# Cross-attention and feed-forward on one core: scores of two slots in one stretch, softmax steps one slot earlier

## The chip, the cores and the metric

The kernel runs on one core of one Trainium2 chip. The metric is the device time of one execution in microseconds (us). Before the change the median of three runs is 498.65 us (498.59 to 500.09).

## What is computed

For each of 8 batches with 512 rows of 256 features, and a context of 1024 rows of 256 of which a mask leaves a short window:

```python
q = (layernorm(x) @ w_q), k = (ctx @ w_k), v = (ctx @ w_v)     # 16 heads of 64
attn = softmax(where(mask, -inf, q @ k.T / 8))
x = x + (attn @ v) @ w_o
w = quantised_int4(kernel)
x = x + layernorm(x) @ w + bias + (layernorm(x) @ a) @ b
```

All of it is in float32 in the reference. The mask is the same for all query rows and hides all but the last keys, so a window of 160 keys per batch (128 and a rest of 32) is enough; the kernel checks this at run time and has a general path that is not taken here.

## The kernel before, in words

Float32 precision is made from float16 halves: a matrix is split into a high half and a low half, and a product is three matmuls (high by high, high by low, low by high). A high half is ScalarE's copy out of PSUM, a low half VectorE's subtraction behind it.

**Slots.** The work is cut into slots. A batch has 16 slots (u = 0 to 15): 4 tiles of 128 rows by 4 groups of 4 heads. 8 batches make LAST = 128 score slots; 12 more slots drain the tail. Every engine goes through the slots in its own function slot(s), one after the other (fast_sp L506, fast_pool L568, fast_act L635, fast_dve L745, fast_pe L919). The engines' queues are in the order of the code; semaphores join them. So the order in which an engine meets its work is written out by hand.

**What a slot k holds before the change.**
- TensorE (L1078): scores(k+2), 12 matmuls of 64 contraction rows by 160 columns in six concurrent pairs (L997), which wait for exponentials of slot k because there are two PSUM buffers for scores; weighted_values(k-3), 16 matmuls of 65 columns (L929, L1018), which wait for the transposed probabilities and for the normalisation of slot k-4, since there is one output bank; then the slot's projection items and its late items.
- VectorE (L885): normalise(k-4) (L878, L879); the first projection item of slot k-1; maxima(k+1) (L812, L816); the other items of slot k-1 (low halves L794, L805, L785, L788; late items L846, L850, L859 to L867, L871).
- ScalarE (L723): the second layer norm's x2 if there is one (L727), exps(k+1) (L682, four activations), then the high halves of slot k's items (L653, L656, L661, L673, L696, L699). exps(k+1) waits for the split of slot k-1.
- GpSimd (L603): split_probs(k), four instructions (L589, L590, L593, L595); in every fourth slot (group 2) the power, the shift and the sum with the bias of a tile's second layer norm (L611, L613, L614), behind VectorE's statistics of the same slot; once a batch a gather and a power for the first layer norm.
- SP (L525): turn_probs(k), the transpose by DMA of the split probabilities into one of TURN_BUFS = 4 buffers, which waits for the weighted values of slot k-4; loads and stores.

The scores, maxima and exponentials of slots 0 to 3 are made ahead of slot 0, between the first projections.

**Items.** Projections for the next batch and late work of older tiles go through three PSUM banks in turn (p_item, LANES = 3): an item waits until the item three before it was evacuated by VectorE (claim, L932). PROJ (L374) lists projections by u: c and x (transposes of the gathered context and of x), k, q, v; FIRST_PROJ is the list of the first batch; h, r0 and r1 come once in four batches. LATE (L384) gives the late items: in group 0 n (transposes of x2), in group 1 w (24 matmuls with w_o), in group 2 f (the feed-forward, 6 matmuls) and o0, in group 3 o1 (transposes of the attention output). VectorE's part of w, here called the w tail, is the residual sum and the tile's statistics.

## Time and profile before

| | |
|---|---|
| median of 3 runs | 498.65 us (498.59 to 500.09) |
| the profiled execution | 499.79 us |
| its span from first to last instruction | 496.5 us |
| mean granted TensorE clock | 0.977 of full speed |
| TensorE busy, matmuls | 449.6 us (91%) |
| VectorE busy | 403.6 us (81%) |
| GpSimd busy | 398.5 us (80%) |
| ScalarE busy | 328.1 us (66%) |

A busy time counts instructions in flight. Matmuls are pipelined and their ends are modelled, so a gap between two matmuls is better read from their starts. A row of a timeline with "x12" is a run of 12 instructions from the start of the first to the end of the last. A bracket at the end of a row gives the idle time before it and the instruction that ended the wait. Slots are numbered here by their place in the kernel: the score group that TensorE computes in slot k is that of slot k+2, and the start of a slot is the start of that group.

### The profile page before, as it was taken

Reading aid. Unit: us, or ns where it says so; the run is one execution under the profiler, and the core shown is the slowest. Engines: PE = TensorE matmul, PEld = TensorE weight load, DVE = VectorE, ACT = ScalarE, POOL = GpSimd, SP = SyncE. Lnnn points to the kernel's source line nnn. Section 1 sums busy time; section 2 is a strip of 40 time slices with the busy share of each in tenths; the row PEclk is TensorE's granted clock in tenths of the full one; section 3 lists DMA queues with packets and bytes.
Section 4 is the critical chain, followed back from the end, with each engine's and each line's share of the span. In section 5 each row is a group of like instructions: output and inputs, shape, how many; then the busy total and the mean of one; then the engine's idle time right before and its main releaser. Section 6 shows DMA issues by size and latency. Waiting matters only on the chain.

```text
span 496.5 us, 15468 instructions
## 1 busy us (share of the span) xinstructions
PE 449.6 (91%) x5855; PEld 326.8 (66%) x5855; DVE 403.6 (81%) x1110; ACT 328.1 (66%) x845; POOL 398.5 (80%) x659
## 2 busy tenths in 40 slices
PE   3777989999999999999999999999999999888884
PEld 1344756786766866777766866687667876566672
DVE  5886689987988989787988989888988888777762
ACT  5977566866577766776677766776677666655621
POOL 5787478999888978788788988798787977889941
PEclk9899799999999999999999999999999999999897
DMA  8602776697957996689758975899777976769971
GB/s 292 207 23 43 141 171 119 127 204 152 172 118 144 197 142 118 125 185 157 147 120 138 196 155 117 150 172 167 139 132 125 164 153 123 146 113 180 165 122 37
DMA packets 218817, 71.91 MB, mean 145 GB/s; under 512 B 202785, under 2 KB 216882, under 8 KB 218738
## 3 DMA queue, kind: packets, MB, share of 16 engines
q1 hardware_dynamic: 217680, 69.25, 73.0%
q0 software_dynamic: 480, 1.31, 0.9%
q8 instruction: 49, 0.80, 0.6%
q10 hardware_dynamic: 578, 0.30, 0.2%
q14 instruction: 30, 0.25, 0.2%
HBM read 14.71 MB, written 4.19 MB: 38 GB/s over the span
## 4 chain that ended last, share of the span: by engine, by line
PE 43%; DVE 26%; ACT 17%; POOL 8%; issue 4%; DMA 1%; DVEq 0%; POOLq 0%; ACTq 0%
PE ps_b L929 32%; ACT arena L682 8%; DVE ps_a L812 7%; PE ps_a L997 6%; DVE arena L805 4%; DVE arena L794 2%; ACT arena L661 2%; DVE arena L879 2%; POOL arena L589 2%; PE ps_b L1055 2%; POOL arena L593 2%; PE ps_b L1018 2%; ACT arena L633 1%; ACT arena L673 1%; DVE arena L816 1%
## 5 line engine op out<-in xcount | busy, mean ns | idle before, releaser
L929 PE MATMUL ps_b<-arena 128*128 128x65 f16 (+3 forms) x3324 | 320.8, 249 | 7.7 <-DVE arena L879 3.4
L929 PEld LDWEIGHTS ps_b<-arena 128*128 128x128 f16 x3324 | 222.0, 99 | 83.1 <-issue 6.4
L682 ACT ACTIVATE arena<-ps_a,arena 128x160 f32<-128x160 f32 x512 | 160.4, 397 | 92.6 <-DVE arena L816 84.1
L593 POOL TENSOR_TENSOR arena<-arena 128x512 f16<-128x512 f32 x128 | 147.9, 1155 | 0.0
L589 POOL CAST arena<-arena 128x512 f16<-128x512 f32 x128 | 78.0, 610 | 54.7 <-ACT arena L682 52.8
L812 DVE TENSOR_REDUCE ps_a<-ps_a 128x4 f32<-128x640 f32 x128 | 105.3, 823 | 0.0
L997 PE MATMUL ps_a<-arena 64*128 64x160 f16 x1536 | 76.5, 233 | 13.2 <-ACT arena L682 13.1
L997 PEld LDWEIGHTS ps_a<-arena 64*128 64x128 f16 x1536 | 50.9, 95 | 38.2 <-issue 20.9
L1018 PE MATMUL ps_b<-arena 128*128 128x65 f16 x512 | 72.1, 194 | 0.0
L879 DVE TENSOR_TENSOR arena<-ps_b,arena 128x256 f32<-128x256 f32 x128 | 54.3, 424 | 4.4
L805 DVE TENSOR_TENSOR arena<-ps_b,arena 128x512 f16<-128x512 f32 x60 | 41.1, 686 | 19.2 <-ACT arena L673 17.8
L699 ACT ACTIVATE arena<-ps_b 128x512 f16<-128x512 f32 x64 | 38.6, 603 | 26.4 <-PE ps_b L1055 26.4
L595 POOL TENSOR_TENSOR arena<-arena 128x128 f16<-128x128 f32 x128 | 54.5, 426 | 0.0
L590 POOL CAST arena<-arena 128x256 f16<-128x256 f32 x128 | 51.1, 399 | 0.0
L1018 PEld LDWEIGHTS ps_b<-arena 128*128 128x128 f16 x512 | 50.4, 99 | 0.0
L846 DVE TENSOR_TENSOR arena<-ps_b,arena 128x512 f16<-128x512 f32 x64 | 43.9, 686 | 5.7 <-DVE mask_u L871 1.0
L673 ACT ACTIVATE arena<-ps_b 128x512 f16<-128x512 f32 x58 | 35.0, 604 | 16.6 <-PE ps_b L929 15.5
L1055 PE MATMUL ps_b<-ident,arena 128*128 128x128 f32 x256 | 38.6, 274 | 0.6 <-DVE arena L879 0.5
L1055 PEld LDWEIGHTS ps_b<-ident,arena 128*128 128x128 f32 x256 | 30.2, 141 | 5.6 <-issue 0.8
L611 POOL TENSOR_TENSOR arena<-arena,neg_half 128x1 f32<-128x1 f32 x32 | 17.7, 552 | 17.4 <-DVE arena L867 17.1
L878 DVE RECIPROCAL arena<-ps_b 128x4 f32<-128x4 f32 x128 | 22.2, 174 | 3.0 <-PE ps_b L1018 2.7
L816 DVE TENSOR_SCALAR arena<-ps_a 128x4 f32<-128x4 f32 x128 | 20.7, 162 | 4.4
(142 smaller groups left out, 423.0 us busy)
## 6 DMA issues: line engine op xcount, KB each, us to landing
arena<-in_x_dram SPq DMA_DIRECT2D x8, 512.0 KB
mask_u<-in_x_dram SPq DMA_DIRECT2D x32, 128.0 KB, 2.9
out_dram<-mask_u SPq DMA_DIRECT2D x32, 128.0 KB, 2.7
arena<-arena SPq DMA_TRANSPOSE x128, 4.0
arena<-arena SPq DMA_DIRECT2D x24, 65.0 KB, 2.7
arena<-in_L_xattn_w_q_dram SPq DMA_DIRECT2D x1, 1024.0 KB, 8.4
arena<-in_L_xattn_w_k_dram SPq DMA_DIRECT2D x1, 1024.0 KB, 10.4
arena<-in_L_xattn_w_v_dram SPq DMA_DIRECT2D x1, 1024.0 KB, 12.0
```

The lines of the kernel that those rows point to most:

```text
L589: nc.gpsimd.tensor_copy(hi_main, main).then_inc(p_hi_made, 1)
L590: nc.gpsimd.tensor_copy(rests[:, :, 0:2, :], rest.unsqueeze(2).broadcast_to([P, GROUP, 2, REST])) \
L593: nc.gpsimd.tensor_tensor(lo_main, main, hi_main, ALU.subtract)
L595: nc.gpsimd.tensor_tensor(rests[:, :, 2, :], rest, rests[:, :, 0, :], ALU.subtract).then_inc(p_lo_made, 1)
L682: ins = nc.scalar.activation(probs[k % 2][:, h, :], p_scores[k % 2][:, h % 2, h // 2 * WINDOW:(h // 2 + 1) * WINDOW], ACT.Exp, bias=neg_ma ...
L805: ins = nc.vector.tensor_tensor(f_q[par][:, 1, j, :], bank[:, :], f_q[par][:, 0, j, :], ALU.subtract)
L812: link(nc.vector.tensor_reduce(p_max[k % 2].rearrange("p (i e) -> p e i", e=2), p_scores[k % 2][:, :, 0:2 * WINDOW].rearrange("p e (i k) - ...
L879: nc.vector.tensor_tensor(attn[k // NG % 2][:, k % NG * GROUP * DH:(k % NG + 1) * GROUP * DH] .rearrange("p (h d) -> p h d", h=GROUP), out ...
L929: mm = nc.tensor.matmul(dst, a, c, start=(first and at == 0), stop=(last and at == n - 1))
L997: mm = nc.tensor.matmul(p_scores[k % 2][:, e, i * WINDOW:(i + 1) * WINDOW], f_q[par][own, q_half, m, t * P:(t + 1) * P], f_k[par][own, k_h ...
L1018: mm = nc.tensor.matmul(dst, turn[:, 2, e, :], vr[par][:, h, :], start=False, stop=True)
L1055: mm = nc.tensor.transpose(bank[:, m * P:(m + 1) * P], attn[tile % 2][:, c * P:(c + 1) * P], ident[:, :])
```

## The change

Scores: TensorE computes scores(k+2) and scores(k+3) one after the other in every even slot k, none in odd slots. Maxima, exponentials, splits and transposes of a slot are moved ahead by one slot, each on its own engine: in slot k VectorE makes maxima(k+2), ScalarE exps(k+2), GpSimd split_probs(k+1), SP turn_probs(k+1). Weighted values stay where they are. A fifth buffer for transposed probabilities is added. The waits inside scores, maxima, exps, split_probs and turn_probs are unchanged.

```diff
@@ -44,7 +44,7 @@
     R = lora_a.shape[1]
     ST, KT, DT, HT = S // P, K // P, D // P, HD // P
     NG = H // GROUP
-    PV_BEHIND, HALF_BUFS, TURN_BUFS = 3, 3, 4
+    PV_BEHIND, HALF_BUFS, TURN_BUFS = 3, 3, 5
     SCALE = DH ** -0.5
     F_EXP = SCALE / (WS * WS)
 
@@ -523,8 +523,10 @@
                     sp.dma_start(vr[batch % 2][REST * i:REST * (i + 1)], src[rows]).then_inc(vr_loaded[batch % 2], 16)
 
             def slot(s):
-                if s.k < LAST:
-                    turn_probs(s.k)
+                if s.k == 0:
+                    turn_probs(0)
+                if s.k + 1 < LAST:
+                    turn_probs(s.k + 1)
                 if s.k == 0:
                     sp.wait_ge(keep_made, 1)
                     sp.wait_ge(zeros_made, 5)
@@ -601,10 +603,10 @@
             norm(2)
 
             def slot(s):
-                if s.k < LAST - 1:
-                    split_probs(s.k)
-                if s.k == LAST - 2:
-                    split_probs(LAST - 1)
+                if s.k == 0:
+                    split_probs(0)
+                if s.k + 1 < LAST:
+                    split_probs(s.k + 1)
                 tile = s.k // NG - 2
                 if s.g == 2 and 0 <= tile < NT:
                     pool.wait_ge(t_var_made, tile + 1)
@@ -726,8 +728,8 @@
                         act.wait_ge(t_rstd_made, tile + 1)
                         nc.scalar.activation(x2, x1, ACT.Identity, bias=t_shift[:, :], scale=t_rstd[:, :]) \
                             .then_inc(x2_made, 1)
-                if DEEP - 1 <= s.k < LAST - 1:
-                    exps(s.k + 1)
+                if DEEP - 2 <= s.k < LAST - 2:
+                    exps(s.k + 2)
                 if s.k == 4:
                     act.wait_ge(ffn_made, 1)
                     nc.scalar.activation(f_ffn_hi, ffn_w[:, :, :], ACT.Copy).then_inc(split_hi, 1)
@@ -890,8 +892,8 @@
                 if b:
                     for i, name in enumerate(b.proj[:first]):
                         item(b, i, name)
-                if DEEP - 1 <= s.k < LAST - 1:
-                    maxima(s.k + 1)
+                if DEEP - 2 <= s.k < LAST - 2:
+                    maxima(s.k + 2)
                 if s.k == 1:
                     ffn_grid(dve)
                 if s.k == 3:
@@ -1076,8 +1078,9 @@
                 mm.then_inc(item_made, 1)
 
             def slot(s):
-                if DEEP - 2 <= s.k < LAST - 2:
+                if DEEP - 2 <= s.k < LAST - 2 and s.k % 2 == 0:
                     scores(s.k + 2)
+                    scores(s.k + 3)
                 if 0 <= s.k - PV_BEHIND < LAST:
                     weighted_values(s.k - PV_BEHIND)
                 for i, name in enumerate(s.proj):
```

## Rows read from the trace of the kernel before

**Rows 1.** Busy time by stretch: us, TensorE, weight loads, VectorE, ScalarE, GpSimd, clock, DMA.

```profile
50.00:450.00 400.00, 383.47 (x5204) 284.00 (x5203) 340.02 (x935) 271.60 (x736) 333.44 (x563) 0.99 0.80 148
```

**Rows 2.** Timeline, TensorE, slots 45 to 49: start us, us, line, operands, count [idle <-releaser].

```profile
200.64 2.78 PE L929 MATMUL ps_b<-arena 128*128 128x256 f16 x24
...
203.35 0.59 PE L997 MATMUL ps_a<-arena 64*128 64x160 f16 x12
...
203.87 0.26 PE L929 MATMUL ps_b<-arena 128*128 128x65 f16 x3
...
212.52 0.44 PE L1069 MATMUL ps_b<-ident,arena 128*128 128x128 f32 x2 [0.63 <-DVE arena L846]
```

**Rows 3.** Timeline, TensorE, slots 50 and 51 (u = 2, 3) to the start of 52.

```profile
217.03 0.59 PE L997 MATMUL ps_a<-arena 64*128 64x160 f16 x12
...
217.55 0.26 PE L929 MATMUL ps_b<-arena 128*128 128x65 f16 x3
...
218.04 0.63 PE L955 MATMUL ps_b<-ident,arena 128*128 128x128 f32 x4
...
218.51 0.82 PE L929 MATMUL ps_b<-arena 128*128 128x256 f16 x6
...
219.70 0.59 PE L997 MATMUL ps_a<-arena 64*128 64x160 f16 x12
...
220.72 1.82 PE L929 MATMUL ps_b<-arena 128*128 128x160 f16 x24
...
222.91 0.59 PE L997 MATMUL ps_a<-arena 64*128 64x160 f16 x12
```

**Rows 4.** Waits, whole span: engine, line, releaser: us in total, times, longest.

```profile
PEld ps_a L997 <- issue: 20.9, 99, 1.0
```

**Rows 5.** Timeline, TensorE, slot 60 (u = 12).

```profile
251.19 0.25 PE L929 MATMUL ps_b<-arena 128*128 128x65 f16 x3 [0.48 <-DVE arena L879]
```

**Rows 6.** Timeline, TensorE, first score matmuls of slots 6 and 18.

```profile
64.87 0.59 PE L997 MATMUL ps_a<-arena 64*128 64x160 f16 x12 [1.12 <-ACT arena L682]
...
103.74 0.59 PE L997 MATMUL ps_a<-arena 64*128 64x160 f16 x12
```

**Rows 7.** Timeline, GpSimd, near the end of the score work.

```profile
439.26 0.55 POOL L611 TENSOR_TENSOR arena<-arena,neg_half 128x1 f32<-128x1 f32 x1 [2.08 <-DVE arena L867]
...
440.71 0.61 POOL L589 CAST arena<-arena 128x512 f16<-128x512 f32 x1
...
443.11 0.61 POOL L589 CAST arena<-arena 128x512 f16<-128x512 f32 x1
```

**Rows 8.** Timeline, VectorE, slots 50 and 51.

```profile
216.50 0.82 DVE L812 TENSOR_REDUCE ps_a<-ps_a 128x4 f32<-128x640 f32 x1
...
217.47 0.42 DVE L859 SCALAR_TENSOR_TENSOR arena<-ps_b,mask_u 128x256 f32<-128x256 f32 x1
...
218.74 0.17 DVE L878 RECIPROCAL arena<-ps_b 128x4 f32<-128x4 f32 x1
...
219.34 0.69 DVE L785 TENSOR_TENSOR arena<-ps_b,arena 128x512 f16<-128x512 f32 x1
...
219.95 0.82 DVE L812 TENSOR_REDUCE ps_a<-ps_a 128x4 f32<-128x640 f32 x1
...
220.92 0.42 DVE L871 TENSOR_TENSOR mask_u<-ps_b,arena 128x256 f32<-128x256 f32 x1
...
221.49 0.69 DVE L846 TENSOR_TENSOR arena<-ps_b,arena 128x512 f16<-128x512 f32 x1
```

**Rows 9.** Timeline, ScalarE, slot 50.

```profile
217.55 1.25 ACT L682 ACTIVATE arena<-ps_a,arena 128x160 f32<-128x160 f32 x4 [1.16 <-DVE arena L816]
...
218.71 0.60 ACT L653 ACTIVATE arena<-ps_b 128x512 f16<-128x512 f32 x1
```

**Rows 10.** Timeline, VectorE, slot 60.

```profile
250.41 0.17 DVE L878 RECIPROCAL arena<-ps_b 128x4 f32<-128x4 f32 x1
...
250.62 0.42 DVE L879 TENSOR_TENSOR arena<-ps_b,arena 128x256 f32<-128x256 f32 x1
```

## The prediction

> **What bounds the kernel now.** I read the busy times by stretch first, then TensorE's instructions in order of time, then the two engines that feed it, then the end.
>
> By stretch: from 50 to 450 us TensorE has a matmul in flight for 383.5 of 400 us, VectorE is busy 340, GpSimd 333, ScalarE 272 [rows 1]. TensorE sets the pace there, but its busy share hides small gaps, so I went on by the starts of its instructions.
>
> In order of time, a score group (12 matmuls) stands once in every slot, between other matmuls. The group at 203.35 lasts 0.59 us, of which its last matmul takes about 0.23, so its 12 starts lie in 0.36, or 0.066 a pair; a seventh pair could start at 0.40, but the weighted values start at 0.52: leaving the group costs 0.12. The 24 matmuls of 256 columns before it take 2.71 from first start to the group's first start; matmuls of 256 columns start 0.109 apart inside the run (2.78 us less the last one's 0.28, by 23), so 24 need 2.62 or 2.63, and entering costs 0.08 [rows 2, 3]. One round trip is 0.20 us; the list of waits has TensorE's weight loads idle 20.9 us before 99 score groups with no releaser, 0.21 each [rows 4]. Apart from that, TensorE stands still at two places of a batch: at the start of a batch (u = 0), where it waits 0.63 us for VectorE's low half of o1, about 1.6 with the gaps around it [rows 2]; and at u = 12, where the weighted values wait 0.54 us for the normalisation before [rows 5]. Thus about 2.15 us of a batch are waits; two batches take 113.3 us (slot 18 at 103.74 to slot 50 at 217.03, [rows 3, 6]), one of the two with the extra items of a quad.
>
> After 440 us it is GpSimd: four instructions of a split take 2.40 us (440.71 to 443.11), the three of a tile's variance 1.45 (439.26 to 440.71), one after the other to the last split [rows 7]; that stretch begins with a wait of 2.08 us.
>
> **The change, part by part.** Times of a slot count from the first score matmul in TensorE's slot; slot 2 of a batch is the worked example.
>
> *Drains.* 62 even slots hold two groups back to back: 62 x 0.20 = 12.4 us less work for TensorE. The second group costs 0.40 to 0.42. The page "TensorEngine Tiling (Array Packing)" of the Trainium skill, section "Tiling Modes", says that changing the tiling mode drains TensorE; rows 2 and 4 agree, and by that rule alone the time would fall by these 12 us.
>
> *What the shift does to VectorE and ScalarE.* Maxima, exponentials, splits and transposes move by one slot together, so their order among each other stays, and the fifth buffer keeps the transposes waiting for the same weighted values as before: no cost there. GpSimd's gather and the two powers of a batch come one split later; they are covered by its idle time, 67 of 400 us [rows 1], some 0.57 a slot, and would cost up to one split (2.40) a batch if a gather came too late. SP issues one transpose more ahead of the first batch's rest values, which weighted values need only in slot 3; later the order on SP is the same. Not so against the scores. Before, maxima found scores that were a slot old: in the example they start at 216.50, 0.53 us *before* the slot's scores [rows 3, 8]. After it, in even slots they need the scores of the same slot, and cannot start before 0.59 + 0.03 = 0.62. On VectorE the second half of all items of the slot before, the normalisation of the next slot and everything behind it stand in line after that wait; on ScalarE every high half of the slot stands behind the exponentials. VectorE's head start of about 1.1 us is gone in every even slot. And odd slots now begin with weighted values, which need that normalisation 0.52 us sooner.
>
> Slots 2 and 3 [rows 3, 8, 9]. VectorE: maxima 0.62, next instruction 0.97 later (1.59), the w tail 1.27 (2.86), the normalisation 0.63 (250.41 to 251.04, [rows 10]) and 0.15 to TensorE (251.04 to 251.19, [rows 5, 10]) = 3.64. TensorE is there at 2.67 + 0.41 - 0.08 = 3.0, so it waits 0.63. ScalarE: exponentials 1.05 after the maxima (216.50 to 217.55), at 1.67, the x1 half 1.16 behind them, 2.84 to 3.44; VectorE's x1 half 3.47 to 4.16; TensorE wants its bank at 4.14 (weighted values 0.49) and gets it at 4.31: 0.17. Maxima 4.08, f 5.05, bank of f free at 5.60; TensorE has k0 (0.83) done at 5.14 and starts k1 at 5.75: 0.61. With k1 and o1 slot 4 begins at 7.1. Before, the pair took 5.88 (217.03 to 222.91). Cost: +1.2 us.
>
> The other pairs by the same steps, after against before: (4,5) 6.52 for 6.72; (6,7) 6.20 for 6.34; (8,9) 7.45 for 7.65; long TensorE items cover VectorE there, and they keep the drain. (10,11) 6.98 for 6.34: w tail and statistics stand behind the maxima, TensorE waits 0.55, 0.15 and 0.13. (12,13) 7.83 for 8.19, the old wait of 0.54 falling to 0.37. (14,15) 6.37 for 6.36. (0,1) 6.97 for 7.32: the wait for o1 stays, since the chain of high half, low half, maxima, exponentials through v0 and v1 is the same; the wait for exponentials becomes one of 0.4 for the normalisation. Together +0.55 us a batch: waits rise from 2.15 to 4.3, drains fall by 1.6. From slot 18 to 112, 5.9 batches and once more a (2,3) pair: **+3.7 us**.
>
> *First batch.* Its projections are packed differently, and slots 8, 10, 14 have little for TensorE in an even slot, so the normalisation is late in slots 9, 11, 13 and 15 (1.4, 1.2, 0.6, 1.1), the second group of slots 6 and 16 waits for exponentials (1.3, 0.75), and 1.0 goes in small ones: 7.4 us, against 2.9 before and 1.2 of drains saved. The stretch from slot 6 to slot 18, 64.87 to 103.74 [rows 6], becomes 42.2 instead of 38.9 us: **+3.3**. Before slot 6 I find +0.1: the exponentials of slot 2 delay the high halves, but VectorE's own work was the limit.
>
> *End.* Where GpSimd is the limit it enters with one split more done: -2.4. The variance of slot 114 comes 0.4 later, since the w tail stands behind maxima, and one group of 1.45 falls behind split 123 rather than ahead of it, but the last tile's statistics can come only after split 127, and the matmuls after them wait for that. **-2.5 us**; nothing and -3.5 are its ends.
>
> Sum: +3.7 + 3.3 + 0.1 - 2.5 = +4.6. The profiled execution took 499.8 us (span 496.5, 3.3 around it), so 504.4 for it; it lies 1.1 above the median of the runs, so I forecast **503.3 us**. The added waits in this sum are 4.6 + 2.5 + 55 x 0.20 = 18.1 us (seven of the 62 drains lie in the last batch, where GpSimd is the limit, and count for nothing). With none of them the time is 485.2, with twice as many 521.4; those are the outer bounds. I take the worked value, since each wait is a sum of measured durations in an order that the code fixes.
>
> **Rivals.** *One: the drains win, because TensorE reaches VectorE's late work later than I think.* Place: the first weighted values and the second and third bank in slots 3 and 11. If half of those waits and of the first batch's arise, 503.3 - 0.5 x (1.4 + 0.8) x 6 - 0.5 x 7.4 = 493; it is faster than before from the point where 4.6 of the 18.1 us of added waits stay away, a quarter of them. For it: VectorE is busy only 85% [rows 1], and slots 5, 9, 13 leave it time. Against: the slack is in other slots than the waits. The Trainium skill's rule of the drain ("TensorEngine Tiling (Array Packing)", section "Tiling Modes") stands for this rival. Chance 0.27.
>
> *Two: the parts cancel*, 498.65 within 0.3%, about what a measurement of this kernel can tell from no change: the waits of slot 3 shrink to half and the end keeps its gain. Chance 0.13.
>
> *Three: worse*, 508 or more: ScalarE, late in each even slot, passes its delay on through the next maxima, or the end brings nothing. Chance 0.08, and the forecast itself 0.52.
>
> *Four: the change does not do what it says*, the second group waiting in mid-stretch for its exponentials in most slots, so that no drain is hidden: I find that only in slots 6, 16 and the last batch; it is inside three.
>
> **How the numbers follow.** Forecast 500.2 to 508 with 0.52, rival one 487 to 497 with 0.27, two 0.13, three 0.08. Rival one lies below 493 with about 0.1, so 493 to 508 leaves out under 0.2; the forecast's own range is 500.5 to 508. Slower by over 0.3% is 0.60, within 0.13, faster 0.27.
>
> **What would show it.** Right: score groups of 24 matmuls about 0.93 us long; no 0.2 us idle in odd slots; in slots u = 3 and u = 11 weighted values waiting for L879 and the next items for VectorE; maxima in even slots not before L997 of the same slot; batches about 0.55 us longer; GpSimd's last split about 2 us sooner after slot 113. Wrong: batches shorter by 1 us or more, or odd slots that begin without a wait.

## The result, and the profile after

The change made the kernel slower: 513.49 us median of 4 runs (512.86 to 514.86) against 499.37 us (498.59 to 501.02, 4 runs on the same chip), ratio 1.0286, 95% interval 1.0257 to 1.0315. The profiled execution took 514.86 us, with a span of 511.6. All times of parts below are from profiled executions.

Busy time of the kernel after by stretch, in the columns of [rows 1]:

```profile
50.00:450.00 400.00, 369.70 (x5003) 276.55 (x5004) 334.00 (x903) 263.26 (x718) 323.89 (x546) 0.99 0.75 143
```

Every engine is busy less than in [rows 1]: TensorE 369.7 of 400 us for 383.5, VectorE 334.0 for 340.0. Nothing became the bound by work; the time went into waiting. Waits of the kernel after, whole span (engine, line, releaser: us in total, times, longest; "..." marks rows, and in the diffs lines, that are left out):

```profile
ACT arena L684 <- DVE arena L818: 138.8, 121, 3.7
...
DVE ps_a L814 <- PE ps_a L999: 35.6, 37, 2.2
PEld ps_b L931 <- issue: 32.2, 45, 1.7
PE ps_b L931 <- DVE arena L881: 22.4, 36, 1.5
...
PEld ps_a L999 <- issue: 12.1, 61, 0.4
```

The last line answers to [rows 4]: the idle time before score groups fell from 20.9 us before 99 groups to 12.1 before 61, so about 9 us of drains did go. The other lines are what came instead. VectorE's maxima (L814) wait 35.6 us for scores, a wait that the kernel before did not have; ScalarE's exponentials (L684) wait 138.8 us for the maxima, 84.1 before; the weighted values (through the helper, L931) wait 22.4 us for the normalisation (L881), 3.4 before; in the pair shown next, the weight loads' wait without a releaser (32.2 us in all) stands in front of the same weighted values.

One steady pair shows it: slots 66 and 67 (u = 2, 3), the ones that the prediction worked out. TensorE in order of time, the columns of [rows 3], from w of slot 65 to the scores of slot 68:

```profile
282.00 2.79 PE L931 MATMUL ps_b<-arena 128*128 128x256 f16 x24 [0.42 <-DVE arena L781]
...
284.72 1.00 PE L999 MATMUL ps_a<-arena 64*128 64x160 f16 x24
285.66 0.26 PE L931 MATMUL ps_b<-arena 128*128 128x65 f16 x3
...
287.28 0.60 PE L1057 MATMUL ps_b<-ident,arena 128*128 128x128 f32 x4
288.39 0.25 PE L931 MATMUL ps_b<-arena 128*128 128x65 f16 x3 [0.51 <-DVE arena L881]
...
290.30 1.00 PE L931 MATMUL ps_b<-arena 128*128 128x160 f16 x12 [0.36 <-DVEq L875]
...
291.67 1.00 PE L999 MATMUL ps_a<-arena 64*128 64x160 f16 x24
```

VectorE in the same two slots, as in [rows 8], and then ScalarE, as in [rows 9]:

```profile
285.36 0.83 DVE L814 TENSOR_REDUCE ps_a<-ps_a 128x4 f32<-128x640 f32 x1 [1.01 <-PE ps_a L999]
...
286.34 0.42 DVE L861 SCALAR_TENSOR_TENSOR arena<-ps_b,mask_u 128x256 f32<-128x256 f32 x1
...
287.61 0.17 DVE L880 RECIPROCAL arena<-ps_b 128x4 f32<-128x4 f32 x1
...
288.19 0.69 DVE L787 TENSOR_TENSOR arena<-ps_b,arena 128x512 f16<-128x512 f32 x1
```

```profile
286.42 1.25 ACT L684 ACTIVATE arena<-ps_a,arena 128x160 f32<-128x160 f32 x4 [2.26 <-DVE arena L818]
287.54 0.61 ACT L655 ACTIVATE arena<-ps_b 128x512 f16<-128x512 f32 x1
```

The 24 score matmuls stand in one run, 0.94 us to the next instruction where two groups took 2 x 0.52. But the maxima start 0.64 after the run began (285.36 - 284.72), not 0.53 before it as in [rows 3, 8]. VectorE stood still for 1.01 us in front of them; the w tail and the normalisation (287.61) come behind, and the weighted values of slot 67 start at 288.39, where the four transposes before them had begun at 287.28 and need 0.47 (218.04 to 218.51 in [rows 3]). Then f's bank holds the second key product (290.30). The pair takes 6.95 us (291.67 - 284.72), 5.88 before.

The start of the span lost time as well. TensorE at slot 4, its two score groups, and then by stretch the gap between them and what follows (columns as in [rows 1]):

```profile
59.33 0.59 PE L999 MATMUL ps_a<-arena 64*128 64x160 f16 x12 [0.50 <-ACT arena L684]
...
62.40 0.98 PE L999 MATMUL ps_a<-arena 64*128 64x160 f16 x12 [2.48 <-ACT arena L684]
```

```profile
61.00:62.40 1.40, 0.01 (x2) 0.01 (x2) 1.33 (x4) 1.31 (x5) 0.96 (x2) 0.65 0.03 6
62.40:68.00 5.60, 4.91 (x44) 3.73 (x45) 3.88 (x11) 2.36 (x7) 4.28 (x7) 0.50 0.70 128
```

The second group waits 2.48 us for the exponentials of the group two before, which hold its buffer, and in the next 5.6 us the granted clock is 0.50, the 1.2 GHz level. The pair (4,5) takes 11.20 us, 6.94 before. What made those exponentials late stands on ScalarE and VectorE just before:

```profile
58.02 1.25 ACT L684 ACTIVATE arena<-ps_a,arena 128x160 f32<-128x160 f32 x4 [3.65 <-DVE arena L818]
59.15 0.78 ACT L658 ACTIVATE arena<-ps_b 128x320 f16<-128x320 f32 x2
```

```profile
59.63 0.49 DVE L790 TENSOR_TENSOR arena<-ps_b,arena 128x320 f16<-128x320 f32 x1 [1.64 <-ACT arena L658]
```

ScalarE makes exponentials first and k0's high half (L658) behind them; VectorE stands still for 1.64 us for that half (L790), its next maxima stand behind, and the exponentials that the second group needs behind those.

Lateness against the kernel before, by the first score matmul of a slot: +3.3 us at slot 2 (where only splits and transposes stand in another slot yet), +1.4 at slot 4, +5.7 at slot 6, +8.1 at slot 18, +16.7 at slot 112, +15.1 at the end of the span. Length of the steady pairs, us, batch from slot 64:

| pair (u) | before | forecast | after | shift alone | high half first |
|---|---|---|---|---|---|
| (0,1) | 7.32 | 6.97 | 7.59 | 7.58 | 7.25 |
| (2,3) | 5.88 | 7.1 | 6.95 | 6.95 | 6.85 |
| (4,5) | 6.72 | 6.52 | 6.57 | 7.00 | 6.58 |
| (6,7) | 6.34 | 6.20 | 6.26 | 6.34 | 6.26 |
| (8,9) | 7.65 | 7.45 | 7.63 | 7.84 | 7.64 |
| (10,11) | 6.34 | 6.98 | 6.90 | 6.91 | 6.47 |
| (12,13) | 8.19 | 7.83 | 8.06 | 8.52 | 8.17 |
| (14,15) | 6.36 | 6.37 | 6.41 | 6.34 | 6.41 |
| batch | 54.8 | 55.4 | 56.4 | 57.5 | 55.6 |

The last two columns are experiments told below.

### The profile page after: what moved, and what is told of

Read it like the earlier page. It is cut to its first block, busy times and chain, and to the rows that moved or that the text cites. A ratio compares the mean times of both kernels' runs of the same rounds, so it can differ in the third digit from the quotient of the medians.

```text
span 511.6 us, 15467 instructions
## 1 busy us (share of the span) xinstructions
PE 449.4 (88%) x5855; PEld 330.3 (65%) x5855; DVE 409.0 (80%) x1110; ACT 324.9 (64%) x845; POOL 398.6 (78%) x659
## 4 chain that ended last, share of the span: by engine, by line
PE 50%; DVE 35%; ACT 10%; issue 3%; DMA 1%; POOL 0%; DVEq 0%; POOLq 0%
PE ps_b L931 38%; DVE ps_a L814 10%; ACT arena L684 6%; PE ps_a L999 6%; DVE arena L881 3%; PE ps_b L1057 2%; DVE arena L848 2%; DVE arena L796 2%; DVE arena L861 2%; ACT arena L663 2%; DVE arena L865 2%; DVE arena L807 2%; DVE arena L818 2%; PE ps_b L1020 1%; DVE mask_u L873 1%
## 5 line engine op out<-in xcount | busy, mean ns | idle before, releaser
L931 PE MATMUL ps_b<-arena 128*128 128x65 f16 (+3 forms) x3324 | 323.9, 248 | 31.9 <-DVE arena L881 22.4
L931 PEld LDWEIGHTS ps_b<-arena 128*128 128x128 f16 x3324 | 224.1, 98 | 110.4 <-issue 32.2
L684 ACT ACTIVATE arena<-ps_a,arena 128x160 f32<-128x160 f32 x512 | 159.5, 394 | 141.2 <-DVE arena L818 138.8
L814 DVE TENSOR_REDUCE ps_a<-ps_a 128x4 f32<-128x640 f32 x128 | 105.6, 825 | 35.6 <-PE ps_a L999 35.6
L999 PE MATMUL ps_a<-arena 64*128 64x160 f16 x1536 | 66.4, 232 | 5.0 <-ACT arena L684 5.0
L999 PEld LDWEIGHTS ps_a<-arena 64*128 64x128 f16 x1536 | 52.2, 95 | 19.2 <-issue 12.1
L881 DVE TENSOR_TENSOR arena<-ps_b,arena 128x256 f32<-128x256 f32 x128 | 54.3, 424 | 4.4
L597 POOL TENSOR_TENSOR arena<-arena 128x128 f16<-128x128 f32 x128 | 54.8, 428 | 0.0
L1057 PEld LDWEIGHTS ps_b<-ident,arena 128*128 128x128 f32 x256 | 28.7, 141 | 9.3 <-DVEq L875 6.5
L616 POOL TENSOR_TENSOR arena<-arena,bias_all 128x256 f32<-128x256 f32 x32 | 23.2, 726 | 0.0
```

The lines of the kernel that those rows point to most:

```text
L597: nc.gpsimd.tensor_tensor(rests[:, :, 2, :], rest, rests[:, :, 0, :], ALU.subtract).then_inc(p_lo_made, 1)
L684: ins = nc.scalar.activation(probs[k % 2][:, h, :], p_scores[k % 2][:, h % 2, h // 2 * WINDOW:(h // 2 + 1) * WINDOW], ACT.Exp, bias=neg_ma ...
L814: link(nc.vector.tensor_reduce(p_max[k % 2].rearrange("p (i e) -> p e i", e=2), p_scores[k % 2][:, :, 0:2 * WINDOW].rearrange("p e (i k) - ...
L881: nc.vector.tensor_tensor(attn[k // NG % 2][:, k % NG * GROUP * DH:(k % NG + 1) * GROUP * DH] .rearrange("p (h d) -> p h d", h=GROUP), out ...
L931: mm = nc.tensor.matmul(dst, a, c, start=(first and at == 0), stop=(last and at == n - 1))
L999: mm = nc.tensor.matmul(p_scores[k % 2][:, e, i * WINDOW:(i + 1) * WINDOW], f_q[par][own, q_half, m, t * P:(t + 1) * P], f_k[par][own, k_h ...
```

## The experiments

Five readings stood against each other in the end. *A*: the maxima that wait for fresh scores hold what is queued behind them on VectorE and ScalarE. *B*: TensorE lost its cover, since odd slots begin with weighted values. *C*: the clock near the start. *D* and *E*, formed on the way: a chain from the fresh scores to the banks, which another order shortens (D), or a lateness that only moves (E).

### Shift and pairing apart

Shift alone: the scores of one slot in every slot, everything else as changed.

```diff
-                if DEEP - 2 <= s.k < LAST - 2 and s.k % 2 == 0:
+                if DEEP - 2 <= s.k < LAST - 2:
                     scores(s.k + 2)
-                    scores(s.k + 3)
```

> The shift without the pairing: maxima, exponentials, splits, transposes one slot ahead as in the changed kernel, but TensorE makes the scores of one slot at the start of every slot. Theory A: the pair of slots u = 2 and 3 takes as long as in the changed kernel (about 7 us), since VectorE sets its end, and the drains come back only in pairs that TensorE sets: 517 to 522 us. Theory B (the pairing, with odd slots that begin with weighted values, is what costs): under 512 us. If the drain of 0.2 us per round trip came back in full: 525.

Measured 520.34 us, ratio 1.0409 (1.0365 to 1.0454): as A expected. Its pair (2,3) is the same 6.95 us as after the change, with two score groups apart: that pair's length is not set by TensorE's work at all. The pairing gives back 6 to 7 us of the 20.6 that the shift costs.

Pairing alone, in the odd slots, where it needs no shift; one edit on the kernel *before*:

```diff
-                if DEEP - 2 <= s.k < LAST - 2:
+                if DEEP - 2 <= s.k < LAST - 2 and s.k % 2:
+                    scores(s.k + 1)
                     scores(s.k + 2)
```

> The kernel before with one edit on TensorE alone: the two score groups k+2 and k+3 of an even slot k are made together at the start of the odd slot k+1, in front of its weighted values. Nothing is shifted on VectorE, ScalarE, GpSimd or SyncE, and four transposed buffers stay. The drains saved are the same; the maxima that wait for fresh scores now stand in odd slots, where the next weighted values come behind w (2.7 us) in four of eight cases. If what the change lost was the shift (a slot of lead paid for at the start, and in each even slot the normalisation behind the fresh maxima with no scores in front of the odd slot's weighted values): no loss before slot 18, waits of about 0.25 us in slots 8 and 0 and 0.6 more than now in slot 12 against 1.6 us of drains, a batch of 54 to 54.6 us, 493 to 499 us. If any two groups made together lose it, wherever they stand, since one of them must be used fresh: batch 55.5 or more, 505 to 512 us.

Measured 501.53 us, ratio 1.0026 (0.9995 to 1.0057), between the two ranges. There is little loss at the start (+0.5 us at slot 17), and 96 slots, 17 to 113, take 331.9 us, 332.4 before. So two groups made together do not cost the 14 us. VectorE's wait for fresh scores is 6.0 us in all for the 35.6 after the change: in odd slots a low half of a projection stands ahead of the maxima, while in slots 2, 6, 10 and 14 w, the only item, stands behind them. Pairs that begin in slots 1, 5, 9 and 13 are 0.2 us shorter, as long as no new wait comes (6.19 for 6.41, 7.02 for 7.23). What the drains bring is given back here, in the batch from slot 65 with more on top (56.2 us for 54.8 before); TensorE in order of time:

```profile
278.73 0.26 PE L929 MATMUL ps_b<-arena 128*128 128x65 f16 x3 [0.49 <-DMA arena<-arena]
...
292.87 0.26 PE L929 MATMUL ps_b<-arena 128*128 128x65 f16 x3 [1.19 <-DMA arena<-arena]
...
307.64 0.25 PE L929 MATMUL ps_b<-arena 128*128 128x65 f16 x3 [1.03 <-DVE arena L879]
```

The weighted values of slots 68 and 72 wait for transposes, those of slot 76 for the normalisation. This run differs from the change in two things, the shift and the parity; even slots without a shift were not tried, since there the second group waits for exponentials made in the same slot.

The fifth buffer:

```diff
-    PV_BEHIND, HALF_BUFS, TURN_BUFS = 3, 3, 5
+    PV_BEHIND, HALF_BUFS, TURN_BUFS = 3, 3, 4
```

> The changed kernel with four transposed buffers instead of five. The transposes that were moved ahead by a slot then wait for the weighted values of their own slot. By the reading that each transposed tile is used three slots later, nothing follows: 512 to 515 us as the changed kernel. If the splits and through them the exponentials are held: over 518 us.

Measured 514.13 us, 1.027 (1.0214 to 1.0326), as the first reading has it: the buffer plays no part that shows.

### Where the waiting step stands

In even slots the maxima behind all items of the slot before:

```diff
-                if DEEP - 2 <= s.k < LAST - 2:
+                if DEEP - 2 <= s.k < LAST - 2 and s.k % 2:
                     maxima(s.k + 2)
...
                         tail_item(b, len(b.proj) + i, name, tile)
+                if DEEP - 2 <= s.k < LAST - 2 and s.k % 2 == 0:
+                    maxima(s.k + 2)
```

> The changed kernel with one thing moved: in even slots VectorE makes the maxima after all its other items of the slot instead of after the first one. Theory A (the maxima of an even slot wait for scores of the same slot, and everything behind them on VectorE and ScalarE waits too): VectorE's waits of L814 for L999, 35.6 us in the changed kernel, fall under 8, TensorE's waits of weighted values for the normalisation, 22.4 us, fall under 10; but the exponentials come about 0.8 us later in even slots and the high halves stand behind them, so part is given back: 505 to 512 us. Theory B (TensorE lost its cover in odd slots, which begin with weighted values, whatever VectorE's order): 512 to 515, the 22.4 us stay above 15. Theory C (the loss is the half clock after new gaps near the start): no change beyond 1.5 us, 512 to 515.

Measured 544.27 us, 1.0881 (1.0823 to 1.0939): every forecast of the time failed. VectorE's wait for scores was gone, as A had said, TensorE's waits for the normalisation stayed at 18.9 us, as B had, and ScalarE's wait for the maxima became

```profile
ACT arena L684 <- DVE arena L818: 191.2, 119, 5.2
```

191.2 us for 138.8. Later maxima are later exponentials, and all high halves of the slot stand behind those. The same for the exponentials, behind ScalarE's high halves, and then both:

```diff
-                if DEEP - 2 <= s.k < LAST - 2:
+                if DEEP - 2 <= s.k < LAST - 2 and s.k % 2:
                     exps(s.k + 2)
...
                         tail_item(s, len(s.proj) + i, name)
+                if DEEP - 2 <= s.k < LAST - 2 and s.k % 2 == 0:
+                    exps(s.k + 2)
```

> The changed kernel with one thing moved: in even slots ScalarE makes the exponentials after the high halves of the slot instead of ahead of them. Theory A: the low half of c at u = 1, which w waits for, comes earlier (0.4 us a batch back), x1 and q4 gain little because VectorE's own line is as late: 509 to 513 us. Theory B and C: 512 to 515.

> Both moves of the two kernels before: in even slots maxima behind VectorE's items, exponentials behind ScalarE's high halves. Theory A: the pair of slots u = 2 and 3 falls from 6.95 to about 6.3 us, a batch by 1 to 1.5 us, the whole to 503 to 508 us. Theory B: at most 2 us better, 511 to 515, waits for L881 above 15 us. Theory C: 512 to 515.

Measured 511.69 us (1.0257, 1.022 to 1.0293) and 508.47 us (1.0182, 1.0148 to 1.0216). With both, pairs (2,3) and (10,11) fell to 6.34 us, near what A expected, but (12,13) rose to 8.82 and (0,1) to 7.75, where the second score group started 1.11 us after the first instead of 0.43: it waited for the exponentials of the slot before. The batch was 56.3 us for 56.4 (56.9 with the exponentials alone), and the gain lay ahead of slot 18: +3.2 us late there, and +2.5 with the exponentials alone, for +8.1. A names the cause of the single pair rightly; that a later place repairs the batch is refuted.

At the start it did repair something. With the exponentials alone behind the high halves, VectorE does not stand still for k0's high half, and TensorE's second group of slot 4 waits 0.74 us, not 2.48:

```profile
59.08 0.59 PE L1001 MATMUL ps_a<-arena 64*128 64x160 f16 x12 [0.74 <-ACT arena L684]
```

The granted clock is 1.00 from 57.75 to 65.31 us in that run, and slots 4 and 5 take 7.6 us for 11.20. That order in the first slots alone was not tried.

### Other orders of VectorE and ScalarE under the shift

In slots 2, 6, 10, 14 the addition that frees w's bank ahead of the maxima, its statistics behind them (`part`); then, with it, the normalisation of the odd slot done in the even one:

```diff
+                if ahead:
+                    tail_item(b, 0, *b.late[0], part=0)
                 if DEEP - 2 <= s.k < LAST - 2:
                     maxima(s.k + 2)
```

```diff
+                if 6 <= s.k < LAST - 2 and s.k % 4 == 2:
+                    normalise(s.k - PV_BEHIND)
...
+                    if 6 <= s.k < LAST - 2 and s.k % 4 == 0:
+                        normalise(s.k - PV_BEHIND)
```

> In each even slot whose VectorE part has the product w of the slot before as its only item (slots 2, 6, 10 and 14 of a batch), the addition that frees w's bank (0.42 us) goes before the maxima that wait for the fresh scores, and the statistics stay behind them: VectorE waited 1.01 us there with w already made. Theory A (the wait for fresh scores holds the rows queued behind it): the wait falls to about 0.6, the divisions by the sums that open the odd slots come 0.4 us earlier, pairs (2,3) and (10,11) lose 0.3 to 0.4 us each, 505 to 510 us. Theory B (in an odd slot TensorE has no scores in front of its weighted values, so anything that VectorE does before the division shows there): the same pairs, but only if the division itself comes earlier; same range. Theory C (half clock after new gaps near the start): no change, 512 to 515.

> The same, and in every even slot from 6 on the division by the sums that opened the odd slot on VectorE is done already in the even slot: behind the maxima in slots 2, 6, 10, 14 of a batch, behind the projection items and ahead of the transposed output in the others. Theory B: TensorE's waits for the division (22.4 us, 36 of them, after the change; 3.4 before it) fall to 3 to 6 us, a batch falls from 56.4 to 54.5 to 55, 498 to 504 us. Theory A: part of it, since exponentials and splits still stand behind the waiting maxima, 504 to 509. Neither (the waits move to the bank claims behind the weighted values): 509 to 514.

Measured 510.29 us (1.0212, 1.013 to 1.0294), just above A's range, and 509.18 us (1.0182, 1.0106 to 1.0257), "the waits move". Pair (10,11) fell from 6.90 to 6.40 and 6.48 us, as A had it; pair (2,3) stayed at 6.95 us in both. With the early normalisation, TensorE and then ScalarE in that pair:

```profile
286.27 1.00 PE L945 MATMUL ps_b<-arena 128*128 128x160 f16 x12 [0.57 <-DVE arena L787]
287.64 1.00 PE L945 MATMUL ps_b<-arena 128*128 128x160 f16 x12 [0.36 <-DVEq L882]
```

```profile
283.76 1.25 ACT L684 ACTIVATE arena<-ps_a,arena 128x160 f32<-128x160 f32 x4 [2.26 <-DVE arena L818]
284.88 0.61 ACT L655 ACTIVATE arena<-ps_b 128x512 f16<-128x512 f32 x1
```

The weighted values no longer wait, and the key product behind them waits 0.57 us for the low half of x1 (L787), which follows the high half (L655), which stands behind the exponentials. B named a wait, not the limit. So D: on ScalarE the first high half ahead of the exponentials in slots 0, 2, 6, 10 and 14, from slot 16 on (with the early addition, and the early normalisation in slots 2, 6, 10, 14 only); then also f's addition ahead of the odd slots' maxima; then also two items ahead of the maxima in slots 0, 4, 8, 12.

```diff
+                for i, name in enumerate(s.proj[:lead]):
+                    item(s, i, name)
                 if DEEP - 2 <= s.k < LAST - 2:
                     exps(s.k + 2)
```

```diff
+                if f_at >= 0:
+                    for i, name in enumerate(b.proj[first:]):
+                        item(b, first + i, name)
+                    tail_item(b, len(b.proj) + f_at, *b.late[f_at])
                 if DEEP - 2 <= s.k < LAST - 2:
                     maxima(s.k + 2)
```

```diff
-                first = 1
+                first = 2 if two else 1
...
+                if o1_first:
+                    tail_item(b, len(b.proj), *b.late[0])
```

> The early addition of w and, in slots 2, 6, 10 and 14 of a batch only, the early division; and on ScalarE the first projection's high half goes before the exponentials in those slots and in slot 0 (from slot 16 on). Theory D, new: what the batch loses is neither the wait for scores nor the division alone but the chain fresh scores, maxima, exponentials, high half, low half, bank free: in the early-division run the keys of slot 3 waited 0.57 us for a bank whose low half stood behind the exponentials, and pair (2,3) stayed at 6.95 us. By D pair (2,3) falls to 6.0 to 6.4, (10,11) to about 6.2 to 6.4, (0,1) to 7.3 or less, the batch to 54.7 to 55.3 us, 500 to 505 us in all. Rival E (the lateness only moves on to the exponentials and from there to the second group of scores of the next pair): the batch stays at 56 or more, 507 to 512 us.

> The same, and in the odd slots 3, 7, 11 and 15 of a batch the addition that frees the bank of the product f goes before the maxima, which in odd slots wait for nothing; the traces before showed 0.36 us of wait for it in slot 3 and a weight load held 0.39 us in slot 7. Theory D: another 0.2 to 0.5 us a batch, 497 to 503 us. Rival E: no better than the run before it, 507 to 512.

> The same, and in slots 0, 4, 8 and 12 of a batch two items instead of one go before the maxima that wait for fresh scores (the second key product, or the transposed output of the slot before). Theory D: the transposes of the normalised tile get their bank earlier (0.2 us in slot 4, up to 1 us in slot 0), batch 53.8 to 54.6, 495 to 501 us. Rival E: the exponentials come 0.6 us later and the second group of scores of the next pair waits, as with all items ahead (544.3 us): 508 to 516 us.

Measured 508.36 us (1.0165, 1.0122 to 1.0208), 517.14 us (1.035, 1.0286 to 1.0413) and 523.41 us (1.048, 1.0431 to 1.053). The first brought (0,1) to 7.25 us as D said, but (2,3) only to 6.85 (D: 6.0 to 6.4). The second is E in plain sight, TensorE's second score group of slots 72 and 76:

```profile
304.86 0.59 PE L1020 MATMUL ps_a<-arena 64*128 64x160 f16 x12 [0.36 <-ACT arena L684]
...
319.53 0.59 PE L1020 MATMUL ps_a<-arena 64*128 64x160 f16 x12 [0.36 <-ACT arena L684]
```

Maxima that wait for nothing were moved back by the 0.42 us of f in odd slots, and the next pair's second group, which needs their exponentials, breaks out of the run. D as a way out fell; E holds.

The one edit for the pair that the forecast had missed most, (0,1): in slot 0 the context's high half ahead of the exponentials.

```diff
+                lead = 1 if s.k and s.u == 0 and s.proj else 0
+                if lead:
+                    item(s, 0, s.proj[0])
                 if DEEP - 2 <= s.k < LAST - 2:
                     exps(s.k + 2)
```

> The changed kernel with one edit on ScalarE: in slot 0 of a batch the high half of the gathered context goes before the exponentials, so that its low half, and with it the bank that w claims in slot 1, come earlier. The prediction had pair (0,1) at 6.97 us, it took 7.59. If that wait is the mis-sized step: 7.2 to 7.3 us, the batch 0.3 us less, 510.5 to 512.5 us. If it only moves: no change, 513 to 515.

Measured 510.06 us, 1.0192 (1.0138 to 1.0246), just under the expected range. Pair (0,1) fell from 7.59 to 7.00 us: w's wait for the context's bank was that step. But (2,3) rose from 6.95 to 7.44, with the weighted values of slot 67 waiting longer:

```profile
286.21 0.25 PE L934 MATMUL ps_b<-arena 128*128 128x65 f16 x3 [0.92 <-DVE arena L884]
```

0.92 us for 0.51. TensorE came sooner, VectorE did not; the batch gained 0.1 us, not the 0.3 expected. Of the 2.8 us by which the span got shorter in the profiled execution (508.8 for 511.6), 1.2 lies ahead of slot 2, and 1.0 between slots 18 and 112.

### The start

The order before through slot 15, the new one from slot 16 (the other engines alike, not shown); then the same with the early addition and normalisation.

```diff
-                if DEEP - 2 <= s.k < LAST - 2:
+                if DEEP - 1 <= s.k <= 16:
+                    maxima(s.k + 1)
+                if 16 <= s.k < LAST - 2:
                     maxima(s.k + 2)
```

> The order of the kernel before through slot 15, the new one from slot 16 on, where maxima, exponentials, splits and transposes of two slots are done at once. If the first batch and the slots before it carry their share of the loss (5 to 8 us of the 14): 505 to 509, lateness at slot 18 from +0 to +3. If what was lost there was only how the clock happened to fall (theory C, no share of the order): 511 to 515.

> Both: the old order through slot 15, and from slot 16 on the early addition and the early division. If the two shares add: 493 to 500, at or below the kernel before. If the loss only moves: 503 to 510.

Measured 510.54 us (1.0221, 1.0141 to 1.03) and 509.41 us (1.0173, 1.0099 to 1.0248). Both miss the range of their first reading; the second lies where "the loss only moves". In the first the lateness is +0.2 us at slot 16 and +4.0 at slot 18; TensorE's score groups there:

```profile
97.21 0.59 PE L1003 MATMUL ps_a<-arena 64*128 64x160 f16 x12 [0.82 <-ACT arena L684]
...
100.25 0.98 PE L1003 MATMUL ps_a<-arena 64*128 64x160 f16 x12 [2.44 <-ACT arena L684]
...
107.79 1.00 PE L1003 MATMUL ps_a<-arena 64*128 64x160 f16 x24
```

The gap of 2.44 us is that of slot 4 after the change (2.48), moved to slot 16, and the granted clock is 0.50 from 100.25 to 105.30 us. Getting a slot ahead cost some 4 us in both places; the run with the exponentials behind the high halves shows that ScalarE's order is part of that price. C is refuted as an independent cause: the clock falls at the gap that the order makes, and not in the run without the gap. What remains chance is the +3.3 us at slot 2. In the other kernels with the changed start slot 2 began anywhere from 49.98 to 53.66 us, and in a kernel told below whose start is that of before (variances later) it began 1.8 us late; the granted clock from 15 to 40 us was 0.80 in that run and after the change, 0.93 before.

### Without the shift, what holds the drains back

On top of the odd pairs: more buffers; then the variances of slot 11 and their power behind slot 12's maxima; the latter on the kernel before alone; and last the normalisation of slots 8, 12 and 0 done behind the fresh maxima of the slot ahead.

```diff
-    PV_BEHIND, HALF_BUFS, TURN_BUFS = 3, 3, 4
+    PV_BEHIND, HALF_BUFS, TURN_BUFS = 3, 4, 5
```

```diff
                     maxima(s.k + 1)
+                if s.norm_ahead and s.u == 12:
+                    norm_var()
...
-                if s.norm_ahead and s.u == 11:
-                    norm_var()
```

```diff
                     maxima(s.k + 1)
+                if early(s.k):
+                    normalise(s.k - PV_BEHIND)
```

> The odd pairs without the shift, with four buffers of split probabilities instead of three and five transposed ones instead of four. In the run without them the steady batch of 56.0 us had lost its drains to new waits: weighted values 0.49 us in slot 4 and 1.19 us in slot 8 for transposes that came late, 1.03 us in slot 12 for the normalisation. If the transposes came late because GpSimd's split waits for the transposes of three groups before to free its buffer (0.75 to 1.18 us in that run): those 1.7 us a batch go, 490 to 496 us. If the queue that issues the transposes is what is late (1.5 to 4 us an issue in that stretch, the rest values among them): 499 to 502 us.

> The same, and the variances of the batch after next (0.9 us on VectorE, at the end of slot 11) and their power on GpSimd go to slot 12, behind its maxima, so that they do not stand ahead of the normalisation that slot 12's weighted values wait for. If that wait (1.03 us, one a batch) goes: 0.5 to 1 us a batch, 3 to 7 us less than the run before it. If it only moves: no difference.

> The kernel before with the variances moved in the same way and nothing else, so that what the pairing is worth can be read from kernels that share this. The kernel before waits 0.49 us there once a batch: 495 to 498 us if it goes, 498 to 501 us if it only moves.

> The odd pairs without the shift, with the larger buffers and the variances moved, and in slots 7, 11 and 15 of a batch (from the second batch on) the normalisation that opens the next even slot is done right behind the fresh maxima, ahead of f and the transposed output. In the run without it TensorE still waited for that normalisation 0.60 us in slot 8, 0.46 in slot 12 and 0.24 in slot 0, 1.3 us of a batch, about as much as the drains bring (1.6). If those waits go and the banks of f and of the transposed output still come in time (their next claims stand 2.7 us and 3.8 us into the pair): batch 54 us or less, 488 to 494 us, below both kernels. If the waits move to the banks, as they did with the shift: 497 to 500 us.

| kernel | us | ratio to before, 95% |
|---|---|---|
| odd pairs, buffers | 500.06 | 1.0006 (0.9979 to 1.0032) |
| and variances later | 498.38 | 0.9977 (0.9952 to 1.0002) |
| before, variances later | 498.35 | 0.9961 (0.9943 to 0.998) |
| odd pairs, all, normalisation early | 496.40 | 0.9928 (0.9899 to 0.9956) |

The buffers took the waits for transposes out of the steady batches (pair (7,8) from 7.91 to 6.95 us where it had been worst), but brought about 1 us by the ratios, which is within their intervals, and not the 6 to 11 expected (96 slots, 17 to 113, took 330.6 us for 331.9); 1.02 us in slot 12 stayed. With the variances later 1.7 us went, not the 3 to 7 expected; one wait of 0.53 us for transposes was back in slot 72, and there were still 0.60, 0.46 and 0.23 us of waits for the normalisation in a batch (slots 56, 60 and 64):

```profile
236.44 0.25 PE L929 MATMUL ps_b<-arena 128*128 128x65 f16 x3 [0.60 <-DVE arena L879]
...
250.62 0.25 PE L929 MATMUL ps_b<-arena 128*128 128x65 f16 x3 [0.46 <-DVE arena L879]
...
264.58 0.25 PE L929 MATMUL ps_b<-arena 128*128 128x65 f16 x3 [0.23 <-DVE arena L879]
```

In the last kernel these are gone; TensorE's only marked waits in the batch from slot 64, to 319 us, are

```profile
265.99 0.63 PE L959 MATMUL ps_b<-ident,arena 128*128 128x128 f32 x4 [0.62 <-ACT arena L689]
...
267.25 0.44 PE L1073 MATMUL ps_b<-ident,arena 128*128 128x128 f32 x2 [0.63 <-DVE arena L846]
...
279.22 1.00 PE L933 MATMUL ps_b<-arena 128*128 128x160 f16 x12 [0.17 <-DVE arena L788]
```

and 96 slots take 326.1 us for 332.4. It is faster than both kernels, by 0.7% against the one before, and misses its expected range by 2.4 us, of which the start, +1.7 us at slot 19, is the larger part. The kernel before with the variances moved has half of that gain without any pair (498.35 us, at the edge of what was expected if its wait goes; pair (12,13) fell from 8.19 to 7.65 us). The two were not run side by side, and no run has the larger buffers and the early normalisation without the pairs, so what the pairs alone bring there is not shown.

## Why the prediction was right or wrong

The direction was right: the forecast was slower, 503.3 us. The size was off by three, and 513.49 lies outside the range of 493 to 508. By the steps:

- **Drains, 0.20 us each:** right. In runs that nothing else holds a pair is 0.21 us shorter (7.02 for 7.23), and a second group starts 0.43 us after the first, forecast 0.40 to 0.42. The Trainium skill's page "TensorEngine Tiling (Array Packing)", section "Tiling Modes", says that a change of the tiling mode drains TensorE, and these runs agree with it; by that rule alone the time would have fallen.
- **The worked pair (2,3), +1.2 us:** right, measured +1.07. The weighted values wait for the normalisation and f's bank holds the second key product, as worked out. (10,11) was forecast at 6.98 and measured 6.90.
- **+0.55 us a batch:** too small; measured +1.57, and the stretch from slot 18 to 112 lost 8.5 us instead of 3.7. (The eight pairs as forecast add up to +0.62, so the sum was 0.07 a batch short of its own terms.) The step that failed is the pair (0,1), "6.97 for 7.32": the text said that the chain through o1 stays and that one wait takes another's place. It missed that w claims the context's bank, and that the context's high half now stands behind exponentials that come late (282.00, 0.42 us for L781); the edit on that one step brought the pair to 7.00 us, the forecast value, but the batch to 56.3 us only, since (2,3) took over most of the wait. The rest is (12,13), 0.23 more than forecast, and (8,9), 0.18: the drains counted as saved there do not show, and what took them was not followed up.
- **"Before slot 6 I find +0.1":** wrong, +5.7 in the profile. 3.3 of it is there at slot 2 already, by chance. Of the rest, 2.4 net (4.3 in slots 4 and 5, less what slots 2 and 3 gave back), the failed step was to see the delay of the high halves and to call VectorE's own work the limit: VectorE stands still for 1.64 us for a high half, the second group of slot 4 for 2.48 us until exponentials are done, and the 5.6 us behind the gap run at half clock. With the exponentials behind the high halves slots 4 and 5 lost 0.6 us, not 4.3. The run with the old start shows the same price at slot 16.
- **First batch +3.3:** measured +2.5 (8.14 - 5.66). The second group of slot 16 came 0.75 us late as forecast; that of slot 6 was not late at all, where 1.3 had been forecast.
- **End -2.5:** measured -1.6. GpSimd's last split starts at 487.43 for 472.44 us, 15.0 later where slot 112 was 16.7 later: 1.7 came back of the 2.4.
- **The fifth buffer and GpSimd at no cost:** right for the buffer (514.13 us with four).

Summed, 5.7 + 2.5 + 8.5 - 1.6 = 15.1 us in the profiled execution where 4.6 was forecast; by the medians it is 14.1. Rival one, that TensorE would come to VectorE's work later than thought, was wrong: it needed a quarter of the added waits to stay away, and more came than were counted. What came true is rival three: ScalarE, late in each even slot, passes its delay on. That it is the shift and not the pairing is shown as far as the odd pairs go. That under the shift no order of VectorE and ScalarE brings the time back is shown for the nine that were tried (508.4 to 544.3 us), not for all.

## What to carry to other kernels

With two buffers, making both at once means that one of them is used fresh; before counting what is saved on the producer, look at what stands ahead of and behind the consumer that will wait, on every in-order queue down to the bank that the producer claims next. If the same pairing can be had in another place, where a consumer has other work ahead of the waiting step and nothing has to be shifted, try that first: here it was one edit on one engine, and about 2 us, hardly clear of the noise, instead of 14. Here the saving on the busiest engine showed only once the waits next in line were moved as well; measure both together, and the moved waits alone.

## What the runs showed that had not been expected

- A gap in TensorE's work had a second price here: after 2.48 us of standing still the granted clock was 0.50 for the next 5.6 us, in which matmuls were in flight for 4.91 us. With the gap at slot 16 instead (2.44 us), slots 4 and 5 took 6.92 us again, and the loss and the 0.50 were there. With a wait of 0.74 us in its place the clock stayed at 1.00.
- The two instructions of the odd maxima, which wait for nothing, moved back behind one of 0.42 us (f), cost 1.0 us a batch (56.6 for 55.6 us) and 9 us in all (517.14 for 508.36), of which the profiled executions show 5.1 between slots 18 and 112.
- Pair (2,3) took 6.94 or 6.95 us in seven kernels, with different waits in it: 0.51 us for the normalisation in one, 0.57 us for a low half in another. Removing the one wait that the profile named there shortened nothing; with VectorE's and ScalarE's step both moved the pair took 6.34 us.
